# A grouped convolution feeding an 8-bit layer: the columns of each conv tile ordered block by block instead of sample by sample

## The reference

```python
def _fake_quant(x, bits, axis):
    bound = float(2 ** (bits - 1) - 1)
    absmax = max(|x|) over axis
    scale = absmax / bound
    return round(clip(x / scale, -bound, bound)) * scale
...
out = conv_general_dilated(x, weight, padding=4, feature_group_count=4)
out = out + (c @ c_weight.T)[:, :, None] + bias[None, :, None]
...
xq, kq = _fake_quant(out, 8, -1), _fake_quant(kernel, 8, 0)
y = xq @ kq + _fake_quant(bias, 16, -1)
return x + _fake_quant(y, 8, -1)
```

## Time and profile before

| what | us |
|---|---|
| median of 3 runs | 250.9 |
| lowest, highest | 250.19, 253.15 |
| the profiled execution | 250.28 |
| its span | 248.2 |
| PE busy | 233.9 |
| DVE busy | 206.7 |
| POOL busy | 191.1 |
| ACT busy | 183.9 |

### The profile page before, as it was taken

How to read it: one execution, slowest core, us unless ns; L and a number is a source line. 1 busy time by engine, 2 the same in 40 slices (tenths; PEclk the granted TensorE clock), 3 DMA queues, 4 the chain that set the end, 5 groups by cost and what they waited for, 6 DMA issues and landing times.

```text
span 248.2 us, 3979 instructions
## 1 busy us (share of the span) xinstructions
PE 233.9 (94%) x1306; PEld 148.8 (60%) x1306; DVE 206.7 (83%) x421; ACT 183.9 (74%) x182; POOL 191.1 (77%) x135
## 2 busy tenths in 40 slices
PE   7799999999999999999999999999999999999920
PEld 4478577756666666566656666665666666656400
DVE  3799897867888898778997897899798979877894
ACT  4589788866777877577598769867897975966652
POOL 4674270339999999889849986995999599989980
PEclk9999999999999999999999999999999999999995
DMA  6996600193227789996889999999989999968938
GB/s 222 399 414 251 254 1 3 17 343 111 86 24 228 171 203 342 200 364 172 170 202 282 193 282 253 248 216 356 209 224 325 241 367 204 284 116 203 417 140 333
DMA packets 16388, 56.29 MB, mean 227 GB/s; under 512 B 2288, under 2 KB 2416, under 8 KB 16368
## 3 DMA queue, kind: packets, MB, share of 16 engines
q1 hardware_dynamic: 11808, 42.08, 46.8%
q0 software_dynamic: 3744, 13.63, 30.9%
q10 hardware_dynamic: 816, 0.33, 0.5%
HBM read 39.26 MB, written 16.78 MB: 226 GB/s over the span
## 4 chain that ended last, share of the span: by engine, by line
PE 87%; DVE 6%; DMA 2%; issue 1%; POOL 1%; ACT 0%; SPq 0%; DVEq 0%
PE dense_ps L691 42%; PE conv_ps L635 35%; PE turn_ps L671 6%; PE small_ps L661 2%; DMA xwin<-x_windows 2%; PE dense_ps L711 1%; DVE a_int L924 1%; DVE y_max L950 1%; DVE small_ps L895 1%; POOL x_lo L324 1%; PE conv_ps L691 1%; DVE y L890 1%; DVE last_max L975 0%; DVE k_max L846 0%; ACT x_hi L441 0%
## 5 line engine op out<-in xcount | busy, mean ns | idle before, releaser
L691 PE MATMUL dense_ps<-kq,a_t 128*128 128x512 bf16 x496 | 115.5, 379 | 0.0
L324 POOL TENSOR_TENSOR x_lo<-xwin,x_hi 128x1032 fp32r<-128x1032 f32 x32 | 81.8, 2571 | 30.1 <-ACT x_hi L441 25.6
L332 POOL TENSOR_TENSOR y<-y,bq 128x512 f32<-128x512 f32 x60 | 81.4, 1448 | 10.9 <-DVE y L881 10.9
L691 PEld LDWEIGHTS dense_ps<-kq,a_t 128*128 128x128 bf16 x496 | 47.2, 100 | 49.0 <-issue 2.0
L895 DVE TENSOR_REDUCE small_ps<-conv_ps 128x8 f32<-128x1024 f32 x32 | 39.3, 1227 | 17.2 <-PE conv_ps L635 17.2
L501 ACT ACTIVATE y_int<-y,y_inv 128x1024 int16<-128x1024 f32 x31 | 35.6, 1148 | 18.0 <-DVE y_inv L936 17.9
L881 DVE SCALAR_TENSOR_TENSOR y<-dense_ps,row_scale,k_scale_b 128x512 f32<-128x512 f32 x58 | 43.1, 745 | 6.0 <-PE dense_ps L691 6.0
L486 ACT CAST a_t<-turn_ps 128x1024 bf16<-128x1024 int16 x32 | 32.3, 1010 | 20.6 <-PE turn_ps L671 20.5
L635 PE MATMUL conv_ps<-x_hi,w_hi 128*128 128x512 f32 x128 | 40.1, 435 | 1.4 <-ACT x_hi L441 1.4
L924 DVE TENSOR_TENSOR a_int<-conv_ps,inv 128x1024 int16<-128x1024 f32 x32 | 39.2, 1224 | 0.0
L441 ACT CAST x_hi<-xwin 128x1032 fp32r<-128x1032 f32 x32 | 33.7, 1053 | 6.4 <-DMA xwin<-x_windows 6.4
(11 more groups left out here) (67 smaller groups left out, 154.6 us busy)
## 6 DMA issues: line engine op xcount, KB each, us to landing
xwin<-x_windows SPq DMA_DIRECT2D x32, 516.0 KB, 6.6
out<-y SPq DMA_DIRECT2D x30, 512.0 KB, 4.2
y<-x_rows POOLq DMA_DIRECT2D x26, 512.0 KB, 7.4
k_raw<-ffn_kernel SPq DMA_DIRECT2D x8, 512.0 KB, 7.8
x_sb<-x_rows SPq DMA_DIRECT2D x6, 512.0 KB, 7.3
w_raw<-taps SPq DMA_DIRECT2D x2, 256.0 KB, 3.3
b_row<-ffn_bias SPq DMA_DIRECT2D x1, 512.0 KB, 10.0
out<-x_sb SPq DMA_DIRECT2D x1, 512.0 KB, 3.1
```

Of the source, the lines that this page charges most:

```text
L324: pool.tensor_tensor(x_lo[:, at].rearrange("p n b -> p (n b)"), xwin[:, t % XWIN, :], x_hi[:, at].bitcast(F32).rearrange("p n b -> p (n b) ...
L332: pool.tensor_tensor(y[:, t % YRING, half(h)], y[:, t % YRING, half(h)], bq[:, half(h)], ALU.add).then_inc(s["biased1" if h else "biased_e ...
L691: mm = pe.matmul(dense_bank(t, h), a_t[:, t % LEVELS, q].rearrange("b j o -> b (j o)"), kq[:, q, half(h)], start=(q == 0), stop=(q == Q - 1))
```

## The change

The columns of the conv are ordered (block, sample) in place of (sample, block): the eight samples of one block lie side by side, in the windows as the host lays them out, in `x_hi` and `x_lo`, and in the accumulator. One matmul's 512 columns are then 64 blocks of 8 samples, one unbroken run of the moving operand that starts at a multiple of 8 elements; the shift `ch` moves it by 8 elements. The seed repeats a row of 8 values over the blocks, in place of each value over its blocks. The column maximum and the levels read the accumulator with a step of 8 elements along the blocks; the levels are written in the same order as before, so everything behind them is the same. No engine's order of instructions changes.

```diff
-NH = HALF // BLOCKS
+BH = HALF // NS
...
-        x_hi = sb("x_hi", [P, XSPLIT, NS, WIN], F32R)
-        x_lo = sb("x_lo", [P, XSPLIT, NS, WIN], F32R)
+        x_hi = sb("x_hi", [P, XSPLIT, WIN, NS], F32R)
+        x_lo = sb("x_lo", [P, XSPLIT, WIN, NS], F32R)
...
         def conv_cols(at):
-            return conv_ps[:, at].rearrange("p h (n b) -> p (h n) b", b=BLOCKS)
+            return conv_ps[:, at].rearrange("p h (b n) -> p (h b) n", n=NS)
...
-                act.copy(conv_cols(t % 2), ctx_cols[:, g, n0:n0 + NS].unsqueeze(2)
-                         .to_broadcast([P, NS, BLOCKS])).then_inc(s["seeded"], 1)
+                act.copy(conv_cols(t % 2), ctx_cols[:, g, n0:n0 + NS].unsqueeze(1)
+                         .to_broadcast([P, BLOCKS, NS])).then_inc(s["seeded"], 1)
...
                             mm = pe.matmul(
-                                conv_ps[:, at, hs, :].rearrange("p (n b) -> p n b", n=NH),
+                                conv_ps[:, at, hs, :],
                                 w[:, ch, g].rearrange("p q o -> p (q o)"),
-                                x[:, x_at, hs * NH:(hs + 1) * NH, ch:ch + BLOCKS],
+                                x[:, x_at, hs * BH + ch:(hs + 1) * BH + ch, :].rearrange("p b n -> p (b n)"),
                                 start=False, stop=False, skip_group_check=True)
...
                 dve.tensor_reduce(cmax_ps,
-                                  conv_ps[:, t % 2].rearrange("p h (n b) -> p (h n) b", b=BLOCKS),
+                                  conv_cols(t % 2).rearrange("p b n -> p n b"),
                                   AX_X, ALU.max, apply_absolute_value=True
                                   ).then_inc(s["col_max_made"], 1)
...
                 dve.tensor_tensor(a_int[:, at, :].rearrange("p (n b) -> p n b", b=BLOCKS),
-                                  conv_cols(at),
+                                  conv_cols(at).rearrange("p b n -> p n b"),
                                   inv8[:, at].unsqueeze(2).to_broadcast([P, NS, BLOCKS]),
                                   ALU.mult).then_inc(s["a_rounded"], 1)
...
-    windows = padded.reshape(N // NS, NS, GROUPS, CG, WIN, Q)[..., ::-1].transpose(0, 2, 5, 3, 1, 4)
+    windows = padded.reshape(N // NS, NS, GROUPS, CG, WIN, Q)[..., ::-1].transpose(0, 2, 5, 3, 4, 1)
...
-        "x_windows": windows.reshape(TILES, P, NS * WIN),
+        "x_windows": windows.reshape(TILES, P, WIN * NS),
```

More of the change, by code:

```diff
@@ L323, in split @@
                 at = t % XSPLIT
-                pool.tensor_tensor(x_lo[:, at].rearrange("p n b -> p (n b)"),
+                pool.tensor_tensor(x_lo[:, at].rearrange("p b n -> p (b n)"),
                                    xwin[:, t % XWIN, :],
-                                   x_hi[:, at].bitcast(F32).rearrange("p n b -> p (n b)"),
+                                   x_hi[:, at].bitcast(F32).rearrange("p b n -> p (b n)"),
                                    ALU.subtract).then_inc(s["lo_made"], 1)
@@ L440, in round_x @@
                 wait(act, "lo_made", t - XSPLIT + 1)
-                act.copy(x_hi[:, t % XSPLIT].rearrange("p n b -> p (n b)"),
+                act.copy(x_hi[:, t % XSPLIT].rearrange("p b n -> p (b n)"),
                          xwin[:, t % XWIN, :]).then_inc(s["hi_made"], 1)
@@ L840, in _ @@
                     dve.wait_ge(s["ctx_made"], 1)
-                    dve.tensor_copy(conv_cols(0), ctx_cols[:, 0, 0:NS].unsqueeze(2)
-                                    .to_broadcast([P, NS, BLOCKS])).then_inc(s["seeded_first"], 1)
+                    dve.tensor_copy(conv_cols(0), ctx_cols[:, 0, 0:NS].unsqueeze(1)
+                                    .to_broadcast([P, BLOCKS, NS])).then_inc(s["seeded_first"], 1)
             def k_maximum(fb):
```

## The result

| | before | after |
|---|---|---|
| median of 22 runs each, us | 250.72 | 249.23 |
| lowest, us | 249.76 | 248.70 |
| span of the profiled execution, us | 248.2 | 247.2 |

The ratio of after to before is 0.9937, with a 95% interval of 0.9915 to 0.9959: 1.6 us less, between 1.0 and 2.1. That is clear of the noise but under the 2% that the prediction took as its bar for "faster", and a fifth of what was forecast (243.5 us).

A forecast was written before the change was run, and what follows sets the result against it. PE's unbroken stretch was taken as the bound. From the profiled 250.28 us, 7.3 us came off for conv matmuls, giving 243.0; 0.4 given back made 243.4, forecast 243.5 us, range 242.0 to 251.5 for 8 in 10.

The forecast's parts named there:

- What bounds the kernel: PE, busy 94% of 248.2 us, runs without a gap from the third tile's conv to the last tile's.
- The moving operand: Conv matmuls of tiles 2 to 31: one unbroken run instead of four saves 360 x 20.2 ns = 7.3 us.
- The argument from L702: Scale matmuls, 4-byte, unbroken, at 111 ns against 56: exactly double, so the broken read likelier causes the conv's 20.2 ns.
- the other side: Forecast case: conv matmuls at 216 to 220 ns, VectorE's reads free, 5.8 to 7.3 us less; chance 50%.
- the width stays: Rival: 4-byte columns can't be fed at full rate, conv matmuls stay at 232 to 238 ns, 250.0 to 251 us; 27%.
- The 0.4 us given back at the end: End of the kernel: 0.4 us of the gain returned, as VectorE, ScalarE and stores run close behind PE.
- VectorE: Column maximum (L895) and levels (L924): stepped accumulator reads taken to cost 0, staying at 1.23 us each.
- its cover: VectorE's slack from 20 to 235 us: 32 us for 60 instructions, 25 us once PE is 7.3 us shorter.
- The bound of 0.37 us a stepped read: L895 and L924: middle bound per 1024-element instruction, from L818's surplus; its rival gave 246 to 250 us, 9%.
- the half-rate rival: L895 and L924 take 2.3 us each when stepped, about 282 us, PE idle before spread and turn; 14%.
- The sentence that 1.04 ns an element is the rate of every VectorE row: VectorE's stepped reads: a gain was excluded because every row runs at 1.04 ns an element, in order or not.
- Seeds, loads, conv result, POOL, DMA: Seeds, loads, conv writes: no change counted; POOL might withhold 0.7 us; a 3% denser DMA stream fits.

The follow-up runs named there:

- Experiment 5: Changed kernel with each conv matmul reading one element of its moving operand 512 times (step of 0): 216 ns a conv matmul, 245.22 us (one run).
- experiment 3: Changed kernel with both parts of windows and conv weights stored as bf16 (2 bytes) instead of the 4-byte type: 216 ns a conv matmul, 243.42 us, ratio to before 0.968.
- experiment 1: Changed kernel with each 512-column conv matmul cut into two of 256, each with its own weight load: 118.2 ns a matmul, 250.25 us (one run).
- experiment 2: Changed kernel with only 64 of the 128 weight columns in each conv matmul: 230 ns a conv matmul, 247.98 us (one run).
- experiment 8: Variant of experiment 3 (2-byte parts) with conv matmuls reading every second element, 4 bytes apart: 226 ns a matmul, 245.86 us (one run).
- experiment 9: Kernel before, with split-window rows padded from 129 to 136 elements so first-shift runs start at multiples of 32 bytes: 249.82 us (one run).
- experiment 12: Changed kernel with one of three conv products in 2-byte type (x_lo as bf16 times a bf16 copy of w_hi): 247.44 us, ratio to before 0.9876.

## Why the prediction was wrong

- *What bounds the kernel*: right. PE runs without a gap before and after, and 348 matmuls of 3.4 ns less are 1.2 us less in the stretch.
- *The moving operand*: this step failed. The sum took 20.2 ns off each of 360 matmuls, as if the whole surplus over a dense matmul were the price of a broken read. It measured 3.4 ns, 1.2 us instead of 7.3. The other 16.6 ns belong to reading 4-byte neighbours at 0.45 ns each, where the 2-byte ones come at 0.42. Experiment 5 shows it from one side (one element over and over: 216 ns), experiment 3 from the other (2-byte elements: 216 ns), and experiments 1 and 2 take the weight load out.
- *The argument from L702*: it was here that the reasoning went astray. L702's matmuls take 111 ns for 128 columns, a whole multiple of the 2-byte time, and the text took that as "4-byte operands add no tail". But 111 ns are 0.87 ns a column, about half the conv's rate, so a read that just falls short of the full rate need not show there. The types differ too: in kernel.py L702's operands (`k_scale`, `ident`) are plain F32 and the conv's are F32R, which the rows both show as f32. The prediction named the first hole ("L702 takes its columns at half the conv's rate") and still gave the other side 50% against 27%. A comparison at half the rate says nothing of a limit on rate.
- *The rival "the width stays"*: nearly right, with its 232 to 238 ns; its "nothing changes" was about 1 us too flat, and the limit isn't the 4-byte type as such (experiments 5 and 8). The measured 249.23 us lie inside the range of 242.0 to 251.5 only because that range took this rival in, not by the sum.
- *The 0.4 us given back at the end*: nothing of it. From the start of the last tile's conv to the end of the span it is 23.6 us before and after.
- *VectorE*: right that its reads cost nothing (1226 and 1224 ns); its cover was never drawn on. The bound of 0.37 us a stepped read, taken from 46 ns of L818, didn't come about: a step of 32 bytes in PSUM costs nothing here. What L818's 46 ns are no run asks. So the half-rate rival fell. The sentence that 1.04 ns an element is the rate of every VectorE row was too broad (L860, from SBUF, takes 744 ns for 1024 elements); that the reads would gain nothing held all the same. The Trainium skill (Advanced Engine Details and Errata, Memory Cachelines) warns of non-contiguous patterns in PSUM, for matmuls; VectorE's reads don't show it (1226 ns against 1227), and the trace agrees with what the Trainium skill (VectorE: DVE Perf Modes, Mode 1x) says of strides and PSUM in the base mode.
- *Seeds, loads, conv result, POOL, DMA*: nothing, as said (L450 1014 ns against 1013).

What the 16.6 ns are in detail is only modelled. One fetch of 8 bytes in about 0.88 ns, a figure taken from the first of these runs, fits the others closely: 4-byte elements 8 bytes apart 453 / 512 = 0.88 ns a column, 2-byte ones 4 bytes apart 226 / 512 = 0.44, 4-byte neighbours 0.45, 2-byte neighbours and a repeated element 0.42. It leaves 6 ns of the 4-byte neighbours, the 461 and 501 ns of wide steps and the order of the twelve places unexplained. That 4-byte elements with a gap between them are simply taken at half the rate would explain the 453 as well; no run parts the two.

## What to carry to other kernels

Before a surplus is put down to the shape of an access, compare with a row of the same type that takes its columns at the same rate. In this PE-bound kernel a conv matmul of 512 columns in the 4-byte reduced type cost 232 to 236 ns where a 2-byte one cost 216; making the low part 2-byte gave about as much again as the reordering. An accumulator may be ordered for PE's sake: VectorE read it with a step of 32 bytes for nothing, while PE stepping through SBUF took twice the time. And read more than one tile before a mean is taken: with a ring of three buffers one piece of the chain can lie 1 to 2% off it.

## What the runs showed of the hardware that was not expected

- PE's moving read: 216 ns for 512 columns of 2-byte neighbours or of one repeated 4-byte element, 226 for 2-byte elements 4 bytes apart, 231 to 232 for 4-byte neighbours, 453, 461 and 501 for 4-byte elements 8, 16 and 516 bytes apart.
- The Trainium skill (Advanced Engine Details and Errata, Memory Cachelines) says of SBUF that two hits on a line of 16 bytes give full performance. 4-byte elements 8 bytes apart hit such a line twice and took 453 ns, and neighbours, with four hits, still not 216: the measurement decides against the rule for PE's moving read.
- A conv matmul's time depends on where its operand starts: 225 to 239 ns from place to place in the changed kernel, repeated within 1 ns every third tile, with the three buffers, from the tenth to the 26th tile.
- In experiment 9, runs that start 4 bytes off a multiple of 32 cost 240 to 246 ns a matmul where those at a multiple took 232 to 235.
- A matmul next to one of the other type is longer: 238 to 239 ns for the last 4-byte one before a 2-byte one, 226 to 229 for the first 2-byte one behind it (changed kernel and experiment 12).
